# Routed experts: weights as the stationary operand, loaded per tile through a ring of six places

## The reference, cut to what matters

```
B, N, C, H, E = (8, 256, 192, 768, 4)
scores = jnp.einsum('bnc,ce->bne', x, gate_w) + gate_b
p_experts = jax.nn.softmax(scores - gate_center, axis=-1)
expert = jnp.argmax(p_experts, axis=-1).reshape(-1)
h = jax.nn.gelu(jnp.einsum('tc,ech->eth', xt, w1) + b1[:, None, :], approximate=False)
out_all = jnp.einsum('eth,ehc->etc', h, w2) + b2[:, None, :]
out = jnp.take_along_axis(out_all, expert[None, :, None], axis=0)[0]
```

## Time and profile before

| | us |
|---|---|
| median of 3 runs | 2609.0 (2608.16 to 2609.42) |
| profiled execution | 2607.57 |
| its span | 2605.8 |
| PE matmul busy | 2256.0 (87%) |
| DVE busy | 1420.5 (55%) |
| ACT busy | 1112.1 (43%) |

### The profile page before, as it was taken

How to read it: one execution, slowest core, us unless ns; L and a number is a source line. 1 busy time by engine, 2 the same in 40 slices (tenths; PEclk the granted TensorE clock), 3 DMA queues, 4 the chain that set the end, 5 groups by cost and what they waited for, 6 DMA issues and landing times. The chain is left out here.

```text
span 2605.8 us, 47552 instructions
## 1 busy us (share of the span) xinstructions
PE 2256.0 (87%) x16381; PEld 2032.9 (78%) x16381; DVE 1420.5 (55%) x3575; ACT 1112.1 (43%) x2070; POOL 867.4 (33%) x758
## 2 busy tenths in 40 slices
PE   0999999999999999999977556199699688877988
PEld 0899999999999999999977445178455466667988
DVE  6566665656666565666645785233376465552222
ACT  0556656565655656565544101011233344532320
POOL 3545455554545545454533221500221000000000
PEclk9999999999999999999988775599899799988999
DMA  1000000000000000000000004200000001016976
GB/s 55 3 4 3 4 3 4 3 3 4 3 4 3 4 3 3 4 3 4 3 3 1 1 0 141 77 15 19 23 14 10 24 36 48 36 48 218 332 238 213
DMA packets 66017, 104.90 MB, mean 40 GB/s; under 512 B 9589, under 2 KB 52255, under 8 KB 64861
## 3 DMA queue, kind: packets, MB, share of 16 engines
q1 hardware_dynamic: 42398, 74.47, 8.6%
q10 hardware_dynamic: 17984, 20.30, 2.4%
q0 software_dynamic: 5568, 9.27, 1.2%
HBM read 75.44 MB, written 28.49 MB: 40 GB/s over the span
## 5 line engine op out<-in xcount | busy, mean ns | idle before, releaser
L255 PE MATMUL banks<-t_wt,t_l 128*128 128x128 f32 x8508 | 1044.5, 276 | 4.1 <-ACT t_l L330 2.9
L255 PEld LDWEIGHTS banks<-t_wt,t_l 128*128 128x128 f32 x8508 | 1013.9, 193 | 18.3 <-ACT t_l L330 4.1
L426 POOL TENSOR_TENSOR t_rstd<-t_var,t_minus_half 128x4 f32<-128x4 f32 (+1 forms) x379 | 366.2, 966 | 628.9 <-DVE t_var L355 628.9
L363 DVE TENSOR_TENSOR t_yn<-banks,t_rstd 128x512 f32<-128x512 f32 (+1 forms) x379 | 249.2, 657 | 344.1 <-POOL t_rstd L426 325.8
L312 ACT ACTIVATE t_sq<-banks 128x512 f32<-128x512 f32 (+1 forms) x379 | 215.8, 569 | 482.2 <-PE banks L255 479.7
L432 POOL TENSOR_TENSOR t_zrstd<-t_zvar,t_minus_half 128x8 f32<-128x8 f32 x196 | 320.4, 1635 | 43.1 <-DVE t_zvar L390 43.1
L343 ACT ACTIVATE t_l<-banks,t_cols 128x512 f32<-128x512 f32 x384 | 292.5, 777 | 48.0 <-PE banks L302 42.0
L352 DVE TENSOR_REDUCE t_ss<-t_sq 128x4 f32<-128x512 f32 (+1 forms) x379 | 244.4, 645 | 112.3 <-ACT t_sq L312 112.3
L330 ACT ACTIVATE t_l<-banks,t_cols 128x512 f32<-128x512 f32 (+2 forms) x381 | 284.6, 747 | 10.9 <-PE banks L264 6.2
L264 PE MATMUL banks<-t_ident,t_yn 128*128 128x128 f32 x1426 | 219.7, 274 | 11.5 <-DVE t_yn L363 10.3
L264 PEld LDWEIGHTS banks<-t_ident,t_yn 128*128 128x128 f32 x1426 | 173.6, 142 | 25.3 <-DVE t_yn L363 11.3
(11 more groups left out here) (314 smaller groups left out, 3401.0 us busy)
## 6 DMA issues: line engine op xcount, KB each, us to landing
t_w<-in_w SPq DMA_DIRECT2D x64, 480.0 KB
ect<-t_ECT SPq DMA_DIRECT2D x16, 750.0 KB, 3.2
t_ectb<-ect ACTq DMA_DIRECT2D x5, 1500.0 KB, 7.9
t_w1x<-in_w1x SPq DMA_DIRECT2D x64, 97.5 KB
ys<-t_ye ACTq DMA_DIRECT2D x64, 96.0 KB
t_yb<-ys ACTq DMA_DIRECT2D x8, 768.0 KB, 10.6
t_ectb<-ect POOLq DMA_DIRECT2D x12, 375.0 KB, 6.7
t_xs<-in_x SPq DMA_DIRECT2D x50, 82.5 KB, 1.8
```

Source lines behind the costliest of these rows:

```text
L255: mm = pe.matmul(psY[bank][:, t * C:(t + 1) * C], src[:, at:at + P], T["wt"][:, 3 * (layer - 1) + k, :], start=(k == 0), stop=(k == 2))
L363: dve.tensor_tensor(T["yn"][:, par, 0:n * C].rearrange("p (t c) -> p t c", c=C), psY[bank][:, 0:n * C].rearrange("p (t c) -> p t c", c=C), ...
L426: pool.tensor_tensor(T["rstd"][:, par, 0:n], T["var"][:, par, 0:n], T["minus_half"][:, 0:n], ALU.pow)\
```

## The change

The hidden activations come out of `up` already turned: w1 is the stationary operand, in twelve products of 128 columns, with the tokens moving. `turn_hidden`, `copy_hidden`, `pGT` and `GT` go. The bias b1 moves into the Gelu's bias, a column of a new tile `b1T`, and so each tile has six Gelus of 128x128 instead of two of 128x384. `down(i)` follows one round after `up(i)` instead of two, and `pX` and `pO` get two banks each. The weights of all experts are no longer loaded in `gate`; each tile's three pieces are loaded by SP into a ring of six places, after a register load of the expert's number on SP. ACT reads that number into a register too, and PE reads it in `down` (for b2) instead of in `up`. Some semaphores are allotted in another list.

```
 # gate, SP
-            for name in ("w1a", "w2", "upper", "steps"):
+            for name in ("upper", "steps"):
                 sp.dma_start(T[name][:], io[name]).then_inc(S["weights_loaded"], 16)
-            sp.dma_start(T["w1b"][HIGH, :], io["w1b"][0:D2, :]).then_inc(S["weights_loaded"], 16)
+            src = bass.AP(io["w1b"].tensor, D2 * N_EXPERT * HID, [[1, P], [P, N_EXPERT * HC], [1, 1]])
+            sp.dma_start(T["b1T"][:, :].rearrange("p (n o) -> p n o", o=1), src, allow_slow_non_contiguous=True)\
+                .then_inc(S["weights_loaded"], 16)
             sp.wait_ge(S["zero_ready"], 3)
-            sp.dma_start(T["w1b"][0:1, :], io["w1b"][D2:D2 + 1, :]).then_inc(S["weights_loaded"], 16)
 # gate, POOL
-            pool.memset(T["w1b"][LOW, :], 0.0).then_inc(S["zero_ready"], 1)
+            pool.memset(T["w1b"][LOW, :, :], 0.0).then_inc(S["zero_ready"], 1)
-            pool.memset(T["eB"][:, :, :], 1.0)
+            pool.memset(T["eB"][:, :, :], 0.0)
 # gate, SP and PE: wait_ge(S["weights_loaded"], 7 * 16) becomes 4 * 16
 # routed_ffn, SP
+            def load_weights(i):
+                slot = i % FFN_RING
+                if i >= FFN_RING:
+                    sp.wait_ge(S["routed_out"], i - FFN_RING + 1)
+                e = sp.value_load(T["expert"][0:1, i:i + 1], min_val=0, max_val=N_EXPERT - 1)
+                hidden = bass.ds(e * HID, HID)
+                done = S[f"ffn_loaded{slot}"]
+                sp.dma_start(w1a[:, slot, :], io["w1a"][:, hidden]).then_inc(done, 16)
+                sp.dma_start(w1b[HIGH, slot, :], io["w1b"][0:D2, hidden]).then_inc(done, 16)
+                sp.dma_start(w2[:, slot, :], io["w2"][:, bass.ds(e * (HC * D), HC * D)]).then_inc(done, 16)
+            for i in range(FFN_RING):
+                load_weights(i)
             sp.wait_ge(S["scattered"], 16 * TILES)
             ...
-            for n in range(len(LOADS)):
-                s = slice(starts[n], starts[n + 1])
-                sp.wait_ge(S["routed_done"], starts[n + 1])
-                sp.dma_start(outs[:, s, :], r[:, s, :]).then_inc(S["routed_stored"], 16)
+            for i in range(FFN_RING, ROUTED):
+                load_weights(i)
+                if i - FFN_RING + 1 in starts:
+                    store(starts.index(i - FFN_RING + 1) - 1)
+            store(len(LOADS) - 1)
 # routed_ffn, PE
             def up(i):
-                expert[i] = pe.value_load(T["expert"][0:1, i:i + 1], min_val=0, max_val=N_EXPERT - 1)
+                slot = i % FFN_RING
+                pe.wait_ge(S[f"ffn_loaded{slot}"], 16 * PARTS_W * (i // FFN_RING + 1))
                 pe.wait_ge(S["rows_copied"], i + 1)
                 if i >= 2:
                     pe.wait_ge(S["hidden"], 2 * (i - 1))
                 for n in range(2):
-                    w = bass.ds(expert[i] * HID + n * HALF_H, HALF_H)
-                    o = pH[i % 2][n][:, 0:HALF_H]
-                    pe.matmul(o, eA[:, i % 2, :], T["w1a"][:, w], start=True, stop=False)
-                    pe.matmul(o, eB[:, i % 2, :], T["w1b"][:, w], start=False, stop=True).then_inc(S["hidden_done"], 1)
+                    for c in range(HC // 2):
+                        o = pH[i % 2][n][:, c * P:(c + 1) * P]
+                        w = slice(n * HALF_H + c * P, n * HALF_H + (c + 1) * P)
+                        pe.matmul(o, w1a[:, slot, w], eA[:, i % 2, :], start=True, stop=False)
+                        mm = pe.matmul(o, w1b[:, slot, w], eB[:, i % 2, :], start=False, stop=True)
+                    mm.then_inc(S["hidden_done"], 1)
             def down(i):
-                pe.wait_ge(S["hidden_copied"], 2 * (i + 1))
-                if i >= 1:
-                    pe.wait_ge(S["routed_done"], i)
+                e = pe.value_load(T["expert"][0:1, i:i + 1], min_val=0, max_val=N_EXPERT - 1)
+                pe.wait_ge(S["hidden"], 2 * (i + 1))
+                if i >= 2:
+                    pe.wait_ge(S["routed_done"], i - 1)
             ...
-            for i in range(ROUTED + 2):
+            for i in range(ROUTED + 1):
                 if i < ROUTED:
                     up(i)
-                if 1 <= i <= ROUTED:
-                    turn_hidden(i - 1)
                 if i + 1 < ROUTED:
                     turn_rows(i + 1)
-                if i >= 2:
-                    down(i - 2)
+                if i >= 1:
+                    down(i - 1)
 # routed_ffn, ACT
             for i in range(ROUTED):
+                if i >= 2:
+                    act.wait_ge(S["routed_out"], i - 1)
+                e = act.value_load(T["expert"][0:1, i:i + 1], min_val=0, max_val=N_EXPERT - 1)
                 for n in range(2):
                     act.wait_ge(S["hidden_done"], 2 * i + n + 1)
-                    if i >= 2:
-                        act.wait_ge(S["hidden_turned"], 2 * (i - 2) + n + 1)
-                    act.activation(G[:, i % 2, n * HALF_H:(n + 1) * HALF_H], pH[i % 2][n][:, 0:HALF_H], ACT.Gelu)\
-                        .then_inc(S["hidden"], 1)
+                    for c in range(HC // 2):
+                        at = n * (HC // 2) + c
+                        ins = act.activation(G[:, i % 2, at * P:(at + 1) * P], pH[i % 2][n][:, c * P:(c + 1) * P], ACT.Gelu,
+                                             bias=T["b1T"][:, bass.ds(e * HC + at, 1)])
+                    ins.then_inc(S["hidden"], 1)
 # routed_ffn, DVE: copy_hidden goes; copy_rows(i + 1), then copy_out(i - 1)
```

More of the change, by code:

```diff
@@ L1164 @@
 LOADS = [3, 6, 6, 6, 6]
+FFN_RING = 6
 def routed_ffn(nc, T, S, io):
     ps = T["ps"]
-    pH, pGT, pX, pO = (ps[0:2], ps[2:4]), ps[4:6], ps[6], ps[7]
-    r, eA, eB, G, GT = T["routed"], T["eA"], T["eB"], T["G"], T["GT"]
+    pH, pX, pO = (ps[0:2], ps[2:4]), (ps[4], ps[5]), (ps[6], ps[7])
+    r, eA, eB, G = T["routed"], T["eA"], T["eB"], T["G"]
+    w1a, w1b, w2, b2 = T["w1a"], T["w1b"], T["w2"], T["b2"]
     HALF_H = HID // 2
+    PARTS_W = 3
     starts = [sum(LOADS[:n]) for n in range(len(LOADS) + 1)]
@@ L1178, in _, with store @@
         def _(sp):
+            def load_weights(i):
[8 more added lines that the diff above has]
+                sp.dma_start(w2[:, slot, :], io["w2"][:, bass.ds(e * (HC * D), HC * D)]).then_inc(done, 16)
+            def store(n):
+                s = slice(starts[n], starts[n + 1])
+                sp.wait_ge(S["routed_done"], starts[n + 1])
+                sp.dma_start(outs[:, s, :], r[:, s, :]).then_inc(S["routed_stored"], 16)
+            for i in range(FFN_RING):
+                load_weights(i)
             sp.wait_ge(S["scattered"], 16 * TILES)
@@ L1238, in down @@
+                    mm.then_inc(S["hidden_done"], 1)
+            def down(i):
+                e = pe.value_load(T["expert"][0:1, i:i + 1], min_val=0, max_val=N_EXPERT - 1)
+                pe.wait_ge(S["hidden"], 2 * (i + 1))
+                if i >= 2:
+                    pe.wait_ge(S["routed_done"], i - 1)
+                o = pO[i % 2][:, 0:D]
                 for c in range(HC):
-                    pe.matmul(pO[:, 0:D], GT[:, i % 2, c * P:(c + 1) * P],
-                              T["w2"][:, bass.ds(expert[i] * (HC * D) + c * D, D)], start=(c == 0), stop=False)
@@ L1241, in down @@
-                pe.matmul(pO[:, 0:D], T["one"][:, :], T["b2"][:, bass.ds(expert[i] * D, D)], start=False, stop=True)\
+                    pe.matmul(o, G[:, i % 2, c * P:(c + 1) * P], w2[:, i % FFN_RING, c * D:(c + 1) * D],
+                              start=(c == 0), stop=False)
+                pe.matmul(o, T["one"][:, :], b2[:, bass.ds(e * D, D)], start=False, stop=True)\
                     .then_inc(S["routed_out"], 1)
             turn_rows(0)
-            for i in range(ROUTED + 2):
+            for i in range(ROUTED + 1):
@@ L1269, in copy_rows @@
                     dve.wait_ge(S["hidden_done"], 2 * (i - 1))
[L1270 to L1277, removed]
-                    dve.tensor_copy(GT[:, i % 2, n * HALF_H:(n + 1) * HALF_H], pGT[n][:, 0:HALF_H])\
-                        .then_inc(S["hidden_copied"], 1)
+                dve.tensor_copy(eA[:, i % 2, :], pX[i % 2][:, 0:P])
+                dve.tensor_copy(eB[D2:P, i % 2, :], pX[i % 2][D2:P, P:2 * P]).then_inc(S["rows_copied"], 1)
             def copy_out(i):
                 dve.wait_ge(S["routed_out"], i + 1)
-                dve.tensor_copy(r[:, i, :], pO[:, 0:D]).then_inc(S["routed_done"], 1)
+                dve.tensor_copy(r[:, i, :], pO[i % 2][:, 0:D]).then_inc(S["routed_done"], 1)
             phi_link = Link(dve, S["phi_link"])
@@ L2011, in program @@
         late_names += ("zero_ready cleared one_ready ffn_var ffn_root scattered ranks_ready expert_ready rows_ready "
-                       "routed_done routed_stored rows_copied rows_turned hidden hidden_done hidden_copied "
-                       "hidden_turned routed_out mix_ahead0 mix_ahead1 mix_ahead2 gathered0 gathered1 gathered2 gathered3 gathered4 gathered5 gathered6 gathered7 routed_loaded0 "
```

(9 more changed lines are left out.)

34 lines of the change are left out of this document (11 added, 23 removed).

## The result

| | median, us | runs | ratio to the kernel before |
|---|---|---|---|
| before | 2608.86 | 4, 2608.16 to 2609.42 | |
| after | 2588.1 | 4, 2585.41 to 2590.36 | 0.9919 [0.9907, 0.9931] |

The change makes the kernel faster by 20.8 us by the medians; 2591.3 was forecast, a gain of 17.7. The median lies on the lower edge of the range (2588), and by the ratio, 0.9919 x 2609.0 = 2587.9, just under it. So the direction and most of the size came as argued, and in these four runs 3 us more came than the sum had. The profiled execution took 2585.41 us with a span of 2583.6.

A forecast was written before the change was run, and what follows sets the result against it. PE was taken to bound the 27 tiles; the period falling from 5.73 to 5.18 us, with end waits gone, gains 17.7 us: 2609.0 - 17.7 = 2591.3 us (chance 0.78), range 2588 to 2600 (its own 2588 to 2595).

The forecast's parts named there:

- the sum of the tiles: 27 tiles: period falls from 5.73 to 5.18 us, last matmul at 1825.13 instead of 1842.79, gain 17.7 us.
- the 1.16 and 0.64 us: PE's waits before tile 2 (for `eB`) and before the last `down` (for `pO`); both were to go.
- Rival C: In `up`: weight loads pace it, 3.91 us and 6.41 a tile, time 2623 us; chance 0.01.
- ACT, DVE and the gate cost nothing: Tiles and gate: six Gelus of 0.37 us fit in 5.18, DVE loses copies, `b1T`'s load is covered; nothing added.
- rival B: In the scatter: weight loads double POOL's 1.49 us per issue, adding 27 us, time 2618; chance 0.03.
- The first six loads: During the scatter: 7.1 MB of weights from near 1638 land by 1666, before rows load from 1677.81; hidden.
- the register load: On PE ahead of each `down`: bounded by 0 and 1.2 us, taken as 0; uncovered in full 32 us.
- rival A: Ahead of each `down`: PE's register load shows, its lead only 1.1 us; at 1.2 a tile 2623.7 us; chance 0.04.
- the ring: Weight stream in the tiles: 1.18 MB per 5.18 us, 228 GB/s, places free four rounds ahead; hidden.
- Rival E: In the tiles: the weight ring starves; at 180 GB/s 6.55 us a tile, time near 2627; chance 0.02.
- the second `pO`: At the end of the tiles: a second output bank removes PE's 0.64 us wait before the last `down`.
- What follows (last copy, store, block end) is unchanged: Behind the tiles' last matmul: nothing changes, so the tiles' 17.7 us is the whole gain.

The follow-up runs named there:

- e4: Kernel after with only the first six weight loads made, later tiles using what lies in their place: 2589.6 us, ratio 0.9922.
- e5: Kernel after with a ring of four places instead of six: 2590.76 us, one run.
- e2: Kernel after, unchanged, measured and profiled a second time: 2591.35 us, ratio 0.9929.
- e3: Kernel before with only the changed semaphore lists (seven names moved): 2609.74 us, ratio 1.0.
- e10: Kernel after with one PSUM bank each for the row transposes and for `down`, instead of two: 2591.57 us, one run.
- e8: Kernel after with b2 added by DVE in the copy out instead of by PE's product: 2582.07 us, ratio 0.9892.
- e7: Kernel after with five register loads on PE ahead of each `down` instead of one: 2628.9 us, one run.
- e11: Kernel after with nine idle PE products ahead of the first tile and nine ahead of the two-way scan: 2588.02 us, ratio 0.9923.
- e9: Kernel after with three register loads on PE ahead of each `down` instead of one: 2596.57 us, one run.

## What the prediction had right, and the step that failed

The median of the first measurement, by its ratio 2587.9, lies just outside the stated range. The mechanism in the tiles was right; what failed is what the forecast said of the stages behind them.

- **Right in mechanism and size: the sum of the tiles.** 17.7 was forecast, the cut spans show 161.8 - 144.1 = 17.7. Its terms: `up` 2.68 (2.68), period 5.18 (5.17 to 5.18), the 1.16 and 0.64 us gone, the 0.78 before tile 1 kept. The price came from rows of the same form, stationary weights with 128 columns moving. Rival C went by the Trainium skill's figures for weight loads before thin products (TensorE: Matmul & The Clock Gate, Back-to-back issue gap), an estimated 3.7 us for `up`; the measured 2.68 disagrees, as the earlier trace rows had.
- **Right: ACT, DVE and the gate cost nothing.** The Gelu at 0.365 us; the scatter 1.50 us apart against rival B's doubling; the rows loaded from 1676.29 (1677.81 before); and `b1T` through in under 5 us. The first six loads landed near 1669 (the DMA share is 0.96 from 1664 to 1668, 0.44 from 1668 to 1672 and 0.23 behind that), some 3 us later than said and 11 before the first `up`. One slip without effect: by the forecast's own terms `down(i)` starts 5.4 us after `up(i)` ends (0.22 + 2.28 + 2.68 + 0.22), not 5.0.
- **Right, and now with a margin: the register load.** Bounded by 0 and 1.2 us and taken as 0. It takes about 0.68 us within a lead of about 1.9 us; rival A's argument, that the lead might be only 1.1, fell.
- **Right: the ring.** Rival E fell: no tile waits, four places are enough, three are not. That the stream leaves PE alone is shown by e4.
- **Right: the second `pO`.** The 0.64 at the end was put down to it; with one bank a wait of 0.54 is back, once, and costs 0.8 us.
- **The step that failed** is "What follows (last copy, store, block end) is unchanged". The stages behind the tiles begin 2.6 us nearer to their first store of ECT in every profile of the kernel after (216.9 twice; 216.7 and 217.0 in e4 and e5), because the clock rises sooner there. The forecast took these stages as fixed in length and had no term for the clock in them. 17.7 + 2.6 = 20.3 us lies within both measurements' intervals: 0.9919 [0.9907, 0.9931] is 18.0 to 24.3 us of 2609, and 0.9929 [0.9916, 0.9943] is 14.9 to 21.9. With 17.7 alone the first would be missed by 0.3. The rest of the distance in the first measurement is no step of the forecast: the profiled execution was 1.6 us ahead before `gate` began, which e2 doesn't repeat.
- **The range failed with it.** It ended at 2588, set by the price of a record alone. It had no term for executions that differ: up to 3 us ahead of the tiles and several in the slot experts and the combination, and medians of the same kernel 3.3 us apart (2588.1 and 2591.35). Three runs within 1.3 us had been read as the spread; 21 had 7.3.
- **Open:** what sets the moment at which the clock rises behind the tiles. It is not the semaphore lists (e3), not the stream of weights (e4), and not the length of the tiles alone, as e10 has nearly the length of the kernel after and the 219.0 of before, and e8 has shorter ones and 218.8. Four variants of the kernel after (e7 to e10) are back at 218.8 to 219.8, so the 2.6 us belong to this one schedule and may go with the next edit. That a sooner rise is worth these us is shown by e11; why this change brings one is not. Open too is why the slot experts take 150.1 us in one profile and 155.2 in another.

A kernel with all weights resident, the stationary tile picked by a register, would need no ring; no run here shows what it would take.

## What to carry to other kernels

In a stage where one engine is busy for all of its time, each record taken off it is worth its distance to the next, priced from a row of the same operation and shape (0.65 us a tile of transposes here, then 0.33 for b2), and a prefetch ring is deep enough once it covers the time from a place's release to its landing (7.0 to 9.3 us here: two rounds of 5.2, not one). Cut both spans at the stage's first and last record and compare the pieces: the forecast's own term can be exact while the total is off by what other stages do. And cut again inside the stage: in e10 a faster start hid a wait at the end. Give the range a term for the other stages, from more runs than three, above all where the granted clock changes level behind the edited stage.

## What the runs showed of the hardware

- A register load on PE takes about 0.68 us (estimate from e7 and e9), and PE's sequencer is about 1.9 us ahead of the array in this loop, so three loads a tile cost only 0.13 us and five cost 1.5.
- Products of 128 columns with a weight load before each ran at 0.112 us in `up`, 4% over what the columns alone took before (0.1075).
- A transfer of 3072 runs of four bytes cost about 10 ns of one engine a run, spread over 16; 86 had been the bound.
- A DMA stream at a share of 0.71 took nothing from a PE that was busy for 133.4 of 134 us: the same stretch takes 136.64 us with it and at a share of 0.07 (e4).
- The same work behind the tiles took 2.6 us more or less by when the granted clock rose, with an edit that touches nothing there, and the slot experts' code took 150.1 to 155.2 us in profiles of different kernels.
